# Counted waits for the first pairs' rows and units of 88 slots in a two-phase mixture-of-experts kernel

## What is computed

```python
router_logits = x @ gate_w                                  # 1024 tokens x 64 experts
top_vals, top_idx = jax.lax.top_k(softmax(router_logits), 8)
rw[token, top_idx] = top_vals / sum(top_vals)
g = einsum('th,ehi->tei', x, w_gate)                        # 256 -> 96
u = einsum('th,ehi->tei', x, w_up)
out = einsum('tei,eih->th', silu(g) * u * rw[:, :, None], w_down)
```

## Time and profile before

| | before |
|---|---|
| median of 3 runs | 365.51 us (364.02 to 365.74) |
| profiled execution | 366.64 us, span 364.9 us |
| mean granted PE clock | 0.894 |
| PE busy | 271.3 us (74%) |
| DVE busy | 242.4 us (66%) |
| POOL busy | 157.3 us (43%) |
| ACT busy | 148.4 us (41%) |
| DMA traffic | 89.63 MB |

### The profile page before, as it was taken

One profiled execution on the slowest core, in us unless ns is written; L12 is line 12 of the kernel. 1 busy time (PEld: TensorE's weight loads), 2 busy tenths in 40 slices (PEclk: granted clock), 3 DMA queues, 4 the chain that ended last, 5 costly groups with the idle time before them and its releaser, 6 DMA issues.

```text
span 364.9 us, 6915 instructions
## 1 busy us (share of the span) xinstructions
PE 271.3 (74%) x1993; PEld 225.5 (62%) x1993; DVE 242.4 (66%) x885; ACT 148.4 (41%) x427; POOL 157.3 (43%) x195
## 2 busy tenths in 40 slices
PE   4898428803775016637899999979999999998852
PEld 1334218702775015526788988968888988886741
DVE  0699999898947845435668997968677776441001
ACT  2145624430664335212444444434444444446700
POOL 4552020300242787777777100000777753337770
PEclk9999999965599555785999999999999999998988
DMA  4899999962890133349999999956999999965532
GB/s 112 297 305 320 286 348 361 332 212 61 252 272 18 70 113 110 112 166 295 372 385 384 379 282 320 345 192 175 265 327 319 331 335 336 316 203 173 170 102 73
DMA packets 46789, 89.63 MB, mean 246 GB/s; under 512 B 8384, under 2 KB 12320, under 8 KB 46752
## 3 DMA queue, kind: packets, MB, share of 16 engines
q10 hardware_dynamic: 20400, 37.95, 32.3%
q1 hardware_dynamic: 20208, 34.45, 29.6%
q0 software_dynamic: 6144, 16.79, 14.3%
HBM read 51.91 MB, written 37.26 MB: 244 GB/s over the span
## 4 chain that ended last, share of the span: by engine, by line
PE 53%; DVE 22%; POOL 11%; issue 5%; DMA 3%; ACT 2%; SPq 1%; POOLq 0%; DVEq 0%; ACTq 0%
PE psum L854 23%; PE psum L862 15%; POOL expert_rows L586 8%; DVE work L1192 6%; PE psum L842 6%; DVE top L1188 5%; PE psum L743 3%; DVE stats L1163 2%; PE psum L732 2%; PE psum L921 2%; POOL xn L645 1%; PE psum L669 1%; POOL rstd L555 1%; DVE xs L1217 1%; POOL pen L645 1%
## 5 line engine op out<-in xcount | busy, mean ns | idle before, releaser
L586 POOL DMA_INDIRECT expert_rows<-x_rows,place_at x64 | 62.7, 979 | 24.5 <-issue 24.5
L1089 ACT ACTIVATE up<-psum 96x96 f32<-96x96 f32 x128 | 31.5, 246 | 80.1 <-PE psum L854 80.1
L1474 DVE TENSOR_TENSOR up<-up,psum 96x96 f32<-96x96 f32 x128 | 32.0, 250 | 39.5 <-ACT up L1089 31.9
L619 POOL DMA_INDIRECT work<-expert_rows,gather_at x32 | 30.3, 947 | 63.5 <-issue 56.1
L1469 DVE COPY silu<-psum 128x192 f32<-128x192 f32 x128 | 45.6, 357 | 16.4 <-PE psum L842 11.4
L842 PEld LDWEIGHTS psum<-ident,gu_w 96*128 96x128 f32 x256 | 36.2, 143 | 29.3 <-DMA gu_w<-expert_rows 10.7
L842 PE MATMUL psum<-ident,gu_w 96*128 96x96 f32 x256 | 43.1, 252 | 11.8 <-DMA gu_w<-expert_rows 9.9
L854 PE MATMUL psum<-silu,wgu 128*96 128x96 f32 x448 | 49.8, 256 | 0.2 <-DVE silu L1469 0.2
L854 PEld LDWEIGHTS psum<-silu,wgu 128*96 128x96 f32 x448 | 45.2, 173 | 0.9 <-DVE silu L1469 0.5
L862 PE MATMUL psum<-proj_t,up 96*96 96x256 f32 x128 | 38.2, 380 | 0.0
L555 POOL TENSOR_TENSOR rstd<-var_eps,minus_half 128x2 f32<-128x2 f32 (+1 forms) x13 | 10.4, 798 | 46.7 <-DVE var_eps L1169 46.6
(11 more groups left out here) (240 smaller groups left out, 580.2 us busy)
## 6 DMA issues: line engine op xcount, KB each, us to landing
expert_rows<-empty_rows ACTq DMA_DIRECT2D x1, 14784.0 KB, 69.2
gu_w<-expert_rows ACTq DMA_DIRECT2D x52, 192.0 KB, 9.5
wgu<-in_L_ffn_w_gate_up SPq DMA_DIRECT2D x21, 384.0 KB, 9.6
expert_rows<-down_w ACTq DMA_DIRECT2D x32, 192.0 KB, 8.1
proj_t<-in_L_ffn_w_down SPq DMA_DIRECT2D x24, 192.0 KB, 10.4
base<-in_L_ffn_w_gate_up SPq DMA_DIRECT2D x6, 384.0 KB
adj<-in_L_ffn_w_gate_up SPq DMA_DIRECT2D x6, 384.0 KB, 5.7
gu_w<-expert_rows SPq DMA_DIRECT2D x12, 192.0 KB, 5.3
```

What stands on the lines that cost most here:

```text
L586: pool.indirect_dma_start(rows_dram, bass.IndirectOffsetOnAxis(ap=place_at[:, t, k:k + 1], axis=0), x_rows[:, t, :], None).then_inc(placed ...
L619: pool.indirect_dma_start(gathered[:, n % G_RING], None, rows_dram[0:X_OVER], bass.IndirectOffsetOnAxis(ap=gather_at[:, t, k:k + 1], axis= ...
L1089: act.activation(silu1[:, u % 2], psum[0:I1, 2 + u % 2, 0:CAP], ACT.Silu).then_inc(silu1_ready, 1)
L1474: dve.tensor_tensor(h1_t[:, u % 2], silu1[:, u % 2], psum[0:I1, 2 + u % 2, CAP:2 * CAP], ALU.mult).then_inc(h_ready, 1)
```

## The change

1. `CAP` goes from 96 to 88 in both phases: tiles, slots, transfers and matmuls that carry slots have 88 where they had 96. The clear's transfer leaves from 88 partitions and has 81 regions in place of 77.
2. The scatters of the first phase run rank by rank (rank 0 of all four tiles, then rank 1, and so on), with a semaphore for each rank. POOL, three scatters after a rank's last one, waits until the rank has landed and raises `picks_done`.
3. DVE and PE count on the chip how many ranks each of the first 12 pairs needs (`last_key`, `count_picks`, two PE fills `F_ORDER`), into `picks_needed`. SP loads the number into a register before each pair's x and waits for `picks_done` to reach it; pair 0 waits for 2.
4. On SP's queue the weights of pairs 15 to 18 pass ahead of the x of pairs 0 to 3, those of pairs 19 and 20 ahead of the x of pairs 4 to 11.
5. Constants that divide by `CAP` change with it (683 to 745, the pair's factor and shift).

```diff
-CAP = 96
+CAP = 88
+SCATTERS_BACK = 3
...
-        placed_a = [sem(f"placed_a{g}") for g in range(TOP_K_EXPERTS // 2)]
+        placed_a = [sem(f"placed_a{k}") for k in range(TOP_K_EXPERTS)]
+        picks_done = sem("picks_done")
+        picks_known = sem("picks_known")
...
+        F_ORDER = [add_fill("order", "dve") for _ in range(2)]
...
             def load_first_rows(p):
                 n = p % X_RING
-                if p < TOP_K_EXPERTS // 2:
-                    sp.wait_ge(placed_a[p], 16 * 2 * HT)
+                if p == 0:
+                    sp.wait_ge(picks_done, 2)
+                else:
+                    if p == 1:
+                        sp.wait_ge(picks_known, 1)
+                    sp.wait_ge(picks_done, sp.value_load(picks_needed[0:1, p:p + 1], min_val=1, max_val=TOP_K_EXPERTS))
+                    sp.sem_inc(over_begun, 1)
...
-            for p in range(X_FIRST):
-                load_first_rows(p)
             sp.wait_ge(bank_filled, F_YT[B - 1] + 1)
             sp.wait_ge(ebias_ready, NT)
             for p in range(15, 19):
                 load_weights(p)
+            for p in range(4):
+                load_first_rows(p)
             sp.wait_ge(x3_ready, NT)
             sp.wait_ge(x_rows_ready, NT)
             for p in range(19, W_RING):
                 load_weights(p)
+            for p in range(4, X_FIRST):
+                load_first_rows(p)
...
+            def picks_landed(n):
+
+                k = (n - SCATTERS_BACK) // HT
+                if n >= SCATTERS_BACK and (n - SCATTERS_BACK) % HT == HT - 1 and k < TOP_K_EXPERTS:
+                    pool.wait_ge(placed_a[k], 16 * HT)
+                    pool.sem_inc(picks_done, 1)
...
-                    g, t, k = n // (2 * HT), n // 2 % HT, 2 * (n // (2 * HT)) + n % 2
-                    if n < 2 * HT and n % (2 * HB) == 0:
+                    t, k = n % HT, n // HT
+                    if n < HT and n % HB == 0:
                         pool.wait_ge(rows_cleared, 16)
...
-                    scatter(t, k, placed_a[g])
+                    scatter(t, k, placed_a[k])
+                    picks_landed(n)
...
             transpose_y0(2)
             transpose_y0(3)
+            begin(F_ORDER[0])
+            pe.wait_ge(place_ready, B // 2)
+            pe.transpose(bank(F_ORDER[0])[0:HT * TOP_K_EXPERTS, 0:P], place8[:, 0:HT].rearrange("p t k -> p (t k)"), ident[:]).then_inc(bank_filled, 1)
+            begin(F_ORDER[1])
+            emptied(pe, F_ORDER[0])
+            pe.matmul(bank(F_ORDER[1])[0:1, 0:HT * TOP_K_EXPERTS], last_key[:], ident[0:HT * TOP_K_EXPERTS, 0:HT * TOP_K_EXPERTS],
+                      start=True, stop=True).then_inc(bank_filled, 1)
...
+            def count_picks():
+
+                farthest, later = over_of[0:1, 0:TOP_K_EXPERTS], list_scratch[0:1, 0, 0:X_FIRST * (TOP_K_EXPERTS - 1)].rearrange("p (n k) -> p n k", n=X_FIRST)
+                filled(F_ORDER[1])
+                dve.tensor_reduce(farthest, bank(F_ORDER[1])[0:1, 0:HT * TOP_K_EXPERTS].rearrange("p (t k) -> p k t", t=HT),
+                                  mybir.AxisListType.X, ALU.max).then_inc(evac["dve"], 1)
+                emptied(dve, F_ORDER[1])
+                link(dve.tensor_tensor(later, farthest[:, 1:].rearrange("p (a k) -> p a k", a=1).to_broadcast([1, X_FIRST, TOP_K_EXPERTS - 1]),
+                                       pair_keys[:], ALU.is_ge))
+                link(dve.tensor_reduce(list_scratch[0:1, 1, 0:X_FIRST], later, mybir.AxisListType.X, ALU.add))
+                dve.tensor_scalar(picks_needed[:], list_scratch[0:1, 1, 0:X_FIRST], 1.0, None, ALU.add).then_inc(picks_known, 1)
...
             for b in (2, 3):
                 add_layer0(b)
                 statistics(2, b)
+            filled(F_ORDER[0])
+            dve.tensor_reduce(last_key[:], bank(F_ORDER[0])[0:HT * TOP_K_EXPERTS, 0:P], mybir.AxisListType.X, ALU.max).then_inc(evac["dve"], 1)
             masked_scores(2)
...
+            count_picks()
             choose_experts(2)
```

More of the change, by code:

```diff
@@ L38 @@
 SUM_FROM = 74
-PAIR_FACTOR = 683
-PAIR_SHIFT = 11
+PAIR_FACTOR = 745
+PAIR_SHIFT = 13
 def gated_layers_kernel(nc, x, ctx_in, mask_ss, mask_bs, g_xattn, g_ffn, wq0, wk0, gamma_raw, gate_up, down,
@@ L194, in gated_layers_kernel @@
         pairs_needed = sb("pairs_needed", [1, HT * TOP_K_EXPERTS], I32)
+        last_key = sb("last_key", [HT * TOP_K_EXPERTS, 1])
+        pair_keys = sb("pair_keys", [1, X_FIRST, TOP_K_EXPERTS - 1])
+        picks_needed = sb("picks_needed", [1, X_FIRST], I32)
         over_of = sb("over_of", [P, 8])
@@ L537, in _ @@
                           channel_multiplier=0, allow_small_or_imprecise_dtypes=True).then_inc(consts_ready, 1)
-            pool.wait_ge(consts_ready, 12)
+            pool.iota(pair_keys[:], [[-PAIR_ROWS, X_FIRST], [0, TOP_K_EXPERTS - 1]], base=OVER_KEYS + 1 + (NP - 1) * PAIR_ROWS,
+                      channel_multiplier=0, allow_small_or_imprecise_dtypes=True).then_inc(consts_ready, 1)
+            pool.wait_ge(consts_ready, 13)
             pool.affine_select(out=before[:], in_=twos_b[:], compare_op=ALU.is_gt, fill=0.0, base=0,
@@ L587, in scatter @@
                                         x_rows[:, t, :], None).then_inc(placed, 16)
+            def picks_landed(n):
[3 more added lines that the diff above has]
+                    pool.sem_inc(picks_done, 1)
             def place_first_half(placed_from, placed_to):
                 for n in range(placed_from, placed_to):
-                    g, t, k = n // (2 * HT), n // 2 % HT, 2 * (n // (2 * HT)) + n % 2
-                    if n < 2 * HT and n % (2 * HB) == 0:
+                    t, k = n % HT, n // HT
+                    if n < HT and n % HB == 0:
                         pool.wait_ge(rows_cleared, 16)
-                        pool.wait_ge(place_ready, n // (2 * HB) + 1)
-                        pool.wait_ge(x_rows_ready, HB * (n // (2 * HB) + 1))
-                    scatter(t, k, placed_a[g])
+                        pool.wait_ge(place_ready, n // HB + 1)
+                        pool.wait_ge(x_rows_ready, HB * (n // HB + 1))
+                    scatter(t, k, placed_a[k])
+                    picks_landed(n)
             place_first_half(0, 2)
@@ L607, in _ @@
             place_first_half(13, HT * TOP_K_EXPERTS)
+            scattered = HT * TOP_K_EXPERTS
             for b in (2, 3):
@@ L613, in _ @@
                         scatter(t, k, placed_b[b - B // 2])
+                        picks_landed(scattered)
+                        scattered += 1
             def gather(n):
@@ L814, in rank_rows @@
                 last.then_inc(bank_filled, 1)
-            pe.wait_ge(consts_ready, 13)
+            pe.wait_ge(consts_ready, 14)
             rank_rows(0)
@@ L1116, in load_rows @@
                     for placed in placed_a:
-                        act.wait_ge(placed, 16 * 2 * HT)
+                        act.wait_ge(placed, 16 * HT)
                 if p == NP:
@@ L1274, in place_rows @@
                 dve.wait_ge(chosen_ready, b + 1)
-                dve.wait_ge(consts_ready, 13)
+                dve.wait_ge(consts_ready, 14)
                 filled(F_RANK[b])
@@ L1337, in list_over @@
                 if step == 0:
-                    link(dve.tensor_scalar(n_over_i[:, 0], n_over[:], 683.0, None, ALU.mult))
+                    link(dve.tensor_scalar(n_over_i[:, 0], n_over[:], 745.0, None, ALU.mult))
                     link(dve.tensor_scalar(n_over_i[:, 1], n_over_i[:, 0], 16, None, ALU.arith_shift_right))
@@ L1422, in find_pairs @@
                     link(dve.tensor_scalar(pick_int[:], place8[:], -1.0 - OVER_KEYS, 0.0, ALU.add, ALU.max))
-                    link(dve.tensor_scalar(pick_int[:], pick_int[:], 6, None, ALU.arith_shift_right))
+                    link(dve.tensor_scalar(pick_int[:], pick_int[:], 4, None, ALU.arith_shift_right))
                 elif step == 1:
```

## The result

The changed kernel takes 389.7 us (388.4 to 391.6, four runs) against 365.6 us before (364.0 to 366.0): ratio 1.0656, interval 1.0614 to 1.0699. It is slower by 24 us; 380 with a range of 351 to 391 was forecast. Its profiled execution took 391.55 us, span 389.8, mean granted clock 0.866.

What follows compares the result with a forecast made beforehand. It took PE's expert loop as the bound, its start held by POOL's scatters and pair 3's x load. Sum: 366.6 - 11.1 - 1.5 + 27 = 381.0, as a median 380, range 351 to 391 us.

Steps and rivals of the forecast that it cites:

- The clear: Zeroing of the rows before POOL's first scatter: forecast to land at 143.5 instead of 95.88, making that scatter 27 us late.
- Equal, on 11 engines of eight rows: How the zeroing's 88 rows spread over DMA engines: eleven equal shares of 1296 KB, against unequal shares on 16.
- The estimate by the Trainium skill's page "SBUF — State Buffer": Alternative for the zeroing: engines paired on ports, 13.6 GB/s each, landing at 131, kernel time 368 us.
- The tenth unit: Expert loop's start: with counted waits the tenth unit's gate and up come at 163.7 instead of 174.82, gaining 11.1 us.
- They cost POOL about nothing: POOL's added waits in the scatters: looking three scatters back, 3.8 us, exceeds a landing's 2.39 us, so almost no cost.
- due after 180: SP's queue: weights of pairs 21 on stand behind the count's wait and are needed only after 180 us; no cost.
- What is late next is DVE: Loop start once pair 3's x wait is gone: DVE's 10.2 us against PE's 7.7 adds 2.5 us by the tenth unit.
- Units of 88: Expert loop: 88 columns for 96 save 13 ns a unit over some 115 units, 1.5 us; other end 8.
- Rival 4: x and y transfers slower on eleven engines: PE could wait 2 to 7 us; adds to any case, no chance given.
- Rival 3: Counted waits do nothing, pair 3 waits to 163.5 as before: 364 us, or 391 with a late zeroing; chance 0.04, split.

## Why the prediction was right or wrong

**The clear: right in mechanism, a little too dear.** "Equal, on 11 engines of eight rows" was the choice that no row decided; the share of 0.68 and the runs with 88, 80 and 96 partitions show it. The first scatter was 22.2 us late, not 27: the clear landed near 138.4, not at 143.5. The pace of 12.1 GB/s that I took for the slow engines was measured as 12.4 (99/8), which makes the landing 133.7 without weights; of the weights' 13.5 us the clear so bore 4.7, less than the half that I took. The Trainium skill's rule in "DMA: Bandwidth & Descriptors" on the number of engines agrees: 88 rows gave 11 engines (share 0.68), 96 gave 16 (1.01), and 80, which 16 divides, landed in 77.1 us. The estimate by the Trainium skill's page "SBUF — State Buffer", 368 us, had 13.6 GB/s for the slow engines; that eight of the eleven are slow and three are through early agrees with the picture of that page of the Trainium skill, but no run here varied which partitions meet at a port, so the ports as the cause remain argued.

**The tenth unit: right.** "Gain 11.1 us" measured 11.05. That it fits so closely is luck in part: from the third unit to the tenth it took 10.9 us, 11.5 in the sum, and from the loop's start to the third 5.2, 4.5 before; the two differences cancel. With units of 96 the gain was 10.2.

**"They cost POOL about nothing": wrong.** That step set three scatters, 3.8 us, against a landing of 2.39 us, one with little other traffic (DMA share 0.43 in 150 to 160 us before, 0.91 after). With the weights moved beside the scatters and x loads between them, landings took up to 6.6 us, and POOL waited 9.1 us in six waits. The landing times of the first half's scatters, as far as the traces give them (least, median, most), after and then before:

```profile
DMA to landing us min/median/max: 2.4/3.8/6.6
DMA to landing us min/median/max: 2.4/2.4/3.5
```

I had named the condition ("were landings later than that, every scatter behind them would slip") and not priced it, though I had counted the moved weights as traffic two paragraphs on. The last scatter's 6.2 us lie beside other weights than the moved ones. SP issues those of pairs 21 to 23 directly behind its x loads, just before that scatter starts at 187.93:

```profile
187.68 0.36 SPq L442 DMA_DIRECT2D wgu<-in_L_ffn_w_gate_up  x1
```

The forecast had them "due after 180" and gave them no effect.

**"What is late next is DVE": incomplete.** After DVE comes ACT's wait for all eight ranks before pair 12, which the diff touches and the sum does not mention. It held nothing before: the last rank had landed by 163.5, and ACT's first x load came at 176.3. With the loop 11 us ahead, it holds the silu, DVE and PE. The two errors are one chain, last rank late and ACT behind it. From the twelfth unit to the fourteenth it is 9.83 us after (189.17 to 199.00) and 2.56 before, so 7.3 us of the 11 go there:

```profile
177.38 0.84 PE L854 MATMUL psum<-silu,wgu 128*96 128x96 f32 x8
...
179.94 0.84 PE L854 MATMUL psum<-silu,wgu 128*96 128x96 f32 x8
```

With units of 96, mending the chain gave 8.2 us (365.3 against 357.1); 1.6 us of that, in the profiled executions, are the clock behind the loop for overfull experts (units 60 to 64: 10.81 and 9.18 us). Most of the rest that the changed kernel's loop lost was 2.7 us of lower clock in three units behind that loop, and 0.8 us where ACT loads that loop's count (1.74 us, 0.51 before).

**Units of 88: right, if for 11 ns and not 13.** From the unit at 293.72 to the one 20 later at 319.08 it is 1.268 us a unit; before, 271.38 to 296.96, 1.279. So 11 ns. After, and then before:

```profile
293.72 0.84 PE L888 MATMUL psum<-silu,wgu 128*96 128x88 f32 x8
...
319.08 0.84 PE L888 MATMUL psum<-silu,xn 128*96 128x88 f32 x8
```
```profile
271.38 0.84 PE L854 MATMUL psum<-silu,wgu 128*96 128x96 f32 x8
...
296.96 0.84 PE L854 MATMUL psum<-silu,xn 128*96 128x96 f32 x8
```

**Rival 4 was no rival but a term.** "PE could wait 2 to 7 us. It adds to any case" stayed out of the sum. Alone the slower transfers cost 8.7 us, in the changed kernel at least the 3.1 us at the end: POOL's gathers of the last rows come after the y stores, and PE waits for them. In the traces that end is 35.4 to 37.3 us with 88-row transfers whole, and 32.1 to 33.6 with 96 rows or with the transfers cut.

The sum so: 366.6 - 11.1 - 1.5 + 22.2 = 376.2 with the clear as measured; 391.55 measured. The 15.3 us between are the gain lost again in the loop and the tail, which the forecast of 380 had covered by its range only. That 389.7 lies inside the range is luck in part: the clear was priced 4.8 us too dear, and the 15.3 us were not priced. Rival 3 with a late clear, 391, comes nearest as a number, but its mechanism did not occur: the counted waits did bring the tenth unit 11 us forward.

## What to carry to other kernels

Before changing a tile's row count, look at every transfer that carries it: with 88 rows, which 16 does not divide, the largest one here took 112 us in place of 69, for 4% fewer bytes. When a wait is taken away, follow every other wait for the same event in all engines' programs, and check the slack of the first that comes after the time you hope to gain. A look back of n instructions is a wait for a landing in the new traffic, not in the old one.

## What the runs showed that I had not expected

- A DMA issue can hold its engine: 0.31 us at the median, up to 2.88 us with 88-row transfers in the busy stretch, and 1.03 us at most in the traces of the runs with 96 rows.
- The same 88-row transfers cost 8.7 us beside the old order of weights and some 3.4 us, an estimate, beside the new one. The old order issues six pairs' weights late, from 169.60 us; whether that is the reason was not tried.
- Two or three units behind the loop for overfull experts ran at 0.50 of the clock in eight of the 14 traces and at full clock in the others, the kernel before among them. That loop took 5.34 us before and 5.71 us in the changed kernel, but 5.34 us also in the run of the counted waits alone, which had the slow units. What decides it stays open.
